# An AdaLN-FFN kernel: byte-packed transposes, weights transposed into SBUF, and new orders on every engine

## What is computed

```python
def fake_quant(x):                      # per row
    s = max(max(|x|) / 127, 1e-8)
    return clip(round(x / s), -127, 127) * s

y = einsum('bij,bkj->bik', x, weight[itok])        # f32 accuracy
h = layernorm(y) * gamma + beta
h = fake_quant(h) @ fake_quant(w1).T + b1
g = gelu(h)
out = x + fake_quant(g) @ fake_quant(w3).T + b3
```

## Time and profile before

| | us |
|---|---|
| median of 3 runs (lowest, highest) | 359.89 (357.31, 361.01) |
| the profiled execution, its own time | 362.2 |
| its span in the trace | 360.4 |
| TensorE busy | 338.1 |
| VectorE, GpSimd, ScalarE busy | 282.6, 264.3, 226.4 |
| mean granted TensorE clock | 0.99 |

### The profile page before, as it was taken

One profiled execution on the slowest core, in us unless ns is written; L12 is line 12 of the kernel. 1 busy time (PEld: TensorE's weight loads), 2 busy tenths in 40 slices (PEclk: granted clock), 3 DMA queues, 4 the chain that ended last, 5 costly groups with the idle time before them and its releaser, 6 DMA issues. The chain is left out here.

```text
span 360.4 us, 5778 instructions
## 1 busy us (share of the span) xinstructions
PE 338.1 (94%) x1854; PEld 234.1 (65%) x1880; DVE 282.6 (78%) x344; ACT 226.4 (63%) x232; POOL 264.3 (73%) x164
## 2 busy tenths in 40 slices
PE   5899999998887999999899999999999999999885
PEld 5788888865753666676665666566666666665442
DVE  0669888879676589798779878788879877979866
ACT  2443668856976567874596468756777478525640
POOL 1503279545997799976999689978997899956840
PEclk9999999999998999999999999999999999999989
DMA  7999986791995399479962999099946990150014
GB/s 240 362 391 411 400 241 122 182 222 56 241 220 128 103 240 215 86 197 260 221 137 87 301 223 202 3 259 260 217 79 166 295 239 0 59 176 1 0 57 177
DMA packets 46203, 67.35 MB, mean 187 GB/s; under 512 B 2918, under 2 KB 37734, under 8 KB 46186
## 3 DMA queue, kind: packets, MB, share of 16 engines
q1 hardware_dynamic: 46186, 67.14, 70.2%
HBM read 58.74 MB, written 8.39 MB: 186 GB/s over the span
## 5 line engine op out<-in xcount | busy, mean ns | idle before, releaser
L1114 PE MATMUL a_ps<-w_hi,x_hi 128*128 128x512 f32 x256 | 106.6, 416 | 1.8 <-ACT y L608 1.7
L1116 PE MATMUL a_ps<-w_hi,x_lo 128*128 128x512 f32 x256 | 100.1, 391 | 0.0
L1115 PE MATMUL a_ps<-w_lo,x_hi 128*128 128x512 f32 x256 | 99.8, 390 | 0.0
L1168 PE MATMUL f_ps<-w_q,q_t 128*128 128x512 bf16 x377 | 89.8, 385 | 3.7 <-ACT q_t L646 2.5
L593 ACT ACTIVATE w_hi<-t_ps 128x1024 fp32r<-128x1024 f32 x48 | 48.3, 1020 | 39.2 <-DVE t_ps L828 39.0
L1168 PEld LDWEIGHTS f_ps<-w_q,q_t 128*128 128x128 bf16 x400 | 37.6, 99 | 51.1 <-issue 7.5
L828 DVE STREAM_TRANSPOSE t_ps<-w_nat 128x1024 f32<-128x1024 f32 x48 | 58.0, 1240 | 14.5 <-DMA w_nat<-in_L_cond_weight 14.4
L834 DVE TENSOR_TENSOR w_lo<-t_ps,w_hi 128x1024 fp32r<-128x1024 f32 x48 | 57.2, 1215 | 4.5 <-ACT w_hi L593 4.3
L1114 PEld LDWEIGHTS a_ps<-w_hi,x_hi 128*128 128x128 f32 x256 | 48.2, 188 | 14.0 <-ACT y L608 3.1
L1116 PEld LDWEIGHTS a_ps<-w_hi,x_lo 128*128 128x128 f32 x256 | 48.0, 188 | 10.6
L1115 PEld LDWEIGHTS a_ps<-w_lo,x_hi 128*128 128x128 f32 x256 | 48.3, 189 | 9.0
(11 more groups left out here) (151 smaller groups left out, 492.1 us busy)
## 6 DMA issues: line engine op xcount, KB each, us to landing
w_nat<-in_L_cond_weight SPq DMA_DIRECT2D x96, 256.0 KB, 6.7
x_res<-in_x SPq DMA_DIRECT2D x7, 1024.0 KB, 7.0
out<-o SPq DMA_DIRECT2D x14, 512.0 KB, 3.0
x_nat<-in_x SPq DMA_DIRECT2D x24, 256.0 KB, 9.6
w_nat<-in_L_cond_weight SPq DMA_DIRECT2D x10, 512.0 KB, 7.2
w_q<-in_L_ffn_w SPq DMA_DIRECT2D x4, 512.0 KB, 10.2
h_r<-in_L_cond_weight SPq DMA_DIRECT2D x4, 512.0 KB, 8.1
w_scale_row<-in_L_ffn_w SPq DMA_DIRECT2D x3, 512.0 KB, 13.3
```

The costliest lines, as they stand in the source:

```text
L1114: pe.matmul(ps, hi, w_hi[:, u, c], start=begin, stop=False)
L1115: pe.matmul(ps, hi, w_lo[:, u, c], start=False, stop=False)
L1116: last = pe.matmul(ps, lo, w_hi[:, u, c], start=False, stop=end)
L1168: last = pe.matmul(ps[:, half, :], q[:, c, :], w[:, c, half_of(half)], start=c == 0, stop=c == CB - 1)
```

## The change

What it does, part by part:

1. **h and g as bytes.** `round_h` and `round_g` write int8 directly (no added constant), into `h_r` viewed as bytes. Two neighbouring bytes are taken as one 16-bit word, so `transpose_tile` needs four blocks in place of eight, and half a bank. `take_h` and `take_g` read the bytes with a stride. Weights keep the old form.
2. **Transposed adapter weights in SBUF.** In the loop `transpose_w` writes `y_first` (SBUF, two buffers) instead of `t_ps`. Both inputs of `low_w` then lie in SBUF, and it is a `scalar_tensor_tensor` with a factor 1.0 in place of a `tensor_tensor`. The same form replaces VectorE's other large sums of two SBUF tensors in the last period.
3. **`t_ps` for the FFN.** Tile 1 of ffn1 and ffn2 uses `t_ps[:, 0]`, h and g transposes use `t_ps[:, 1]`, so tiles 0 and 1 no longer share banks.
4. **Scale rows through DRAM.** `store_scales` writes `wq_scale` to a scratch tensor, `load_scale_row` reads it back broadcast; `scale_row` and `take_scale_row` are gone.
5. **Start.** The first unit's hi·hi matmuls wait only for `w_hi`. DMA issues, TensorE, ScalarE, VectorE and GpSimd are in a new order.
6. **Last period.** New order; its normalisers skip two small instructions; the last half of the last tile is computed, finished and stored in two quarters of 256 columns.

```diff
+            if isinstance(b, int) and b == 2:
+                return t_ps[:, k].rearrange("p b k -> p (b k)").rearrange("p (c n) -> p c n", n=LOADED)
+            return y_first[:, k].rearrange("p (c n) -> p c n", n=LOADED)
...
+            return t_ps[:, 0] if t == 1 and not (isinstance(f, int) and f == 0) else f_ps[:]
...
-                dve.tensor_tensor(part_of_unit(w_lo, u, k), piece_bank(k), part_of_unit(w_hi, u, k).bitcast(F32),
-                                  ALU.subtract).then_inc(w_lo_ready, 1)
+                dve.scalar_tensor_tensor(part_of_unit(w_lo, u, k), piece_buffer(b, k), 1.0,
+                                         part_of_unit(w_hi, u, k).bitcast(F32), ALU.mult, ALU.subtract
+                                         ).then_inc(w_lo_ready, 1)
...
-                act.activation(a[:, t, :], a[:, t, :], ACT.Identity, scale=g_inv[:, t:t + 1], bias=magic[:]
-                               ).then_inc(g_rounded, 1)
+                act.activation(g_8[t], a[:, t, :], ACT.Identity, scale=g_inv[:, t:t + 1]).then_inc(g_rounded, 1)
...
-                for c in range(CB):
-                    last = pe.transpose(blocks[:, c, :], halves[:, c * P:(c + 1) * P], ident_16[:])
+                words = src.bitcast(BF16)
+                for c in range(CB // PACK):
+                    last = pe.transpose(blocks[:, c, :], words[:, c * P:(c + 1) * P], ident_16[:])
...
+                sp.dma_start(scale_scratch[n].rearrange("(i p) -> p i", p=P), wq_scale[:, RT * n:RT * (n + 1)],
+                             allow_slow_non_contiguous=True
+                             ).then_inc(scales_stored[n], 16)
...
+                sp.dma_start(w_scale_row[:, n, :], scale_scratch[n:n + 1, :].broadcast_to([P, D])
+                             ).then_inc(scale_row_loaded[n], 16)
...
             def period(p):
-                piece(p, 2, 0)
                 transpose_h(p - 1, 0)
                 transpose_h(p - 1, 1)
+                piece(p, 2, 0)
                 piece(p, 2, 1)
-                ffn1(p - 1, 0)
                 piece(p, 3, 0)
                 piece(p, 3, 1)
+                ffn1(p - 1, 0)
                 ffn1(p - 1, 1)
                 piece(p + 1, 0, 0)
+                piece(p + 1, 0, 1)
+                piece(p + 1, 1, 0)
                 transpose_g(p - 1, 0)
-                piece(p + 1, 0, 1)
+                piece(p + 1, 1, 1)
+                transpose_g(p - 1, 1)
                 ffn2(p - 1, 0)
-                piece(p + 1, 1, 0)
-                transpose_g(p - 1, 1)
-                piece(p + 1, 1, 1)
                 ffn2(p - 1, 1)
```

More of the change, by code:

```diff
@@ L8 @@
 BF16 = mybir.dt.bfloat16
+I8 = mybir.dt.int8
 I16 = mybir.dt.int16
@@ L130, in adaln_ffn_kernel @@
         x_rows = {0: o, 13: x_last}
+        bytes_of = [h_r[:, t, :].bitcast(I8) for t in range(TT)]
+        h_8 = [row[:, 0:D] for row in bytes_of]
+        g_8 = [row[:, D:2 * D] for row in bytes_of]
+        g_8_last = [row[:, 2 * D:3 * D] for row in bytes_of]
+        scale_scratch = nc.dram_tensor("scale_scratch", (2, D), F32, kind="Internal").ap()
         a_ps = psum("a_ps", [P, TT, BANK])
@@ L982, in rescale_and_bias_half @@
                     dve.wait_ge(last_half_scaled, half + 1)
-                    dve.tensor_tensor(part, part, b1_row[:, half_of(half)], ALU.add).then_inc(last_half_biased, 1)
+                    dve.scalar_tensor_tensor(part, part, 1.0, b1_row[:, half_of(half)], ALU.mult, ALU.add
+                                             ).then_inc(last_half_biased, 1)
                 def max_half(half):
@@ L1117, in products, with first_unit_piece @@
                 return last
+            def first_unit_piece(k):
+                pe.wait_ge(first_hi_ready, first_piece(1, k) + 1)
+                for t in range(TT):
+                    tokens = slice(t * P, (t + 1) * P)
+                    for c in range(CP * k, CP * (k + 1)):
+                        pe.matmul(a_ps[:, t, :], x_hi[:, c, tokens], w_hi[:, 0, c], start=c == 0, stop=False)
+                pe.wait_ge(first_lo_ready, first_piece(1, k) + 1)
+                for t in range(TT):
+                    tokens = slice(t * P, (t + 1) * P)
+                    for c in range(CP * k, CP * (k + 1)):
+                        pe.matmul(a_ps[:, t, :], x_hi[:, c, tokens], w_lo[:, 0, c], start=False, stop=False)
+                        last = pe.matmul(a_ps[:, t, :], x_lo[:, c, tokens], w_hi[:, 0, c], start=False, stop=False)
+                if k == 1:
+                    last.then_inc(w_used, 1)
             def piece(b, u, k):
                 kh, ch = divmod(u, CH)
+                if isinstance(b, int) and b == 0 and u == 0:
+                    first_unit_piece(k)
+                    return
                 if isinstance(b, int) and b == 0:
@@ new lines, in ffn2_last, with ffn2_last_quarter @@
+                def ffn2_last(t, half):
+                    pe.wait_ge(g_t_ready, TT * LAST + t + 1)
+                    if t == 0:
+                        pe.wait_ge(ffn1_scaled, KH * TT * LAST + half + 1)
+                    else:
+                        pe.wait_ge(last_half_scaled, half + 1)
+                    product_half(q_last[:, 1, t], w_q[1], (t_ps[:, 1], f_ps)[t], half, ffn2_done)
+                def ffn2_last_quarter(n):
+                    pe.wait_ge(last_half_scaled, KH)
+                    if n == 1:
+                        pe.wait_ge(last_o_scaled, 1)
+                    for c in range(CB):
+                        last = pe.matmul(last_quarter(n), q_last[:, 1, 1, c, :],
+                                         w_q[1][:, c, D - BANK // 2 * (2 - n):D - BANK // 2 * (1 - n)],
+                                         start=c == 0, stop=c == CB - 1)
+                    last.then_inc(ffn2_done, 1)
@@ L1376, in _ @@
             prepare((13,))
-            piece(2, 0, 1)
+            piece(2, 0, 0)
             prepare((14,))
             prepare((15,))
+            piece(2, 0, 1)
+            transpose_g(0, 0)
             piece(2, 1, 0)
-            scale_row(1)
+            ffn2(0, 0)
             piece(2, 1, 1)
-            transpose_g(0, 0)
-            ffn2(0, 0)
             transpose_g(0, 1)
```

614 lines of the change are left out of this document (344 added, 270 removed).

## The result

The changed kernel takes 390.07 us (median of 4 runs, 389.55 to 392.99), the kernel before 358.6 on the same chip: ratio 1.085 [1.080, 1.090]. I had said 343, faster. It is slower by 31 us, and outside my range, which went up to 368.

The account below looks back on a forecast made before the run. A loop period was taken as TensorE's own work plus about 1.1 us of waiting. 362.2 - 5.2 (start) - 6.5 (five periods) - 5.1 (last period) - 0.7 (last store) = 344.7, less 2.3, 342.4; said 343, range 336 to 368.

Parts of the forecast that it names:

- the middle kind: Loop, `low_w`: only GpSimd instructions beginning inside one wait; 1.6 us a period for GpSimd, 0.4 us charged to the period.
- My own bounds: Loop, eight `low_w` a period: cost between nothing and 7.0 us of GpSimd plus 16.8 us of VectorE.
- the other pair: Last period of the old trace: two VectorE `tensor_tensor`, 4.53 us against 2 x 1.2, waited about 2.1 us for GpSimd.
- The second rival: Loop: shared reads of `low_w` slow GpSimd, period 42 us, median 365; with VectorE waiting too 43.5 and 373; chance 0.20.
- The list of TensorE: Loop: TensorE's own work in a period, 37.6 us before, falls by 0.9 to 36.7 us.
- Bytes at 0.9 us a period: Loop: four transposed blocks instead of eight for each of four tiles take 0.9 us a period off TensorE.
- The 0.3 and 0.4 us: Loop: waits added per period, 0.3 us for ScalarE's late chain, 0.4 for GpSimd slowed by `low_w`; period 37.4 us.
- The start: Before the loop: -1.9 scale rows, -0.9 bytes, -2.6 waits, -1.7 slow stretch, +1.9 `prepare` steps and conversions; sum -5.2 us.
- the lower bound: Start, scale rows through DRAM: the scatter's price lies between nothing and the start's whole gain; nothing was taken.
- The last period: From 309.34: -1.8 transposes, -2.7 wait for `take_g`, -1.6 slow clock, 1.0 given back for the new order; -5.1 us.
- The last store: End: it waits for a quarter of the columns instead of half, saving about half of VectorE's 0.75 and 0.69: -0.7 us.
- The transpose into SBUF: Loop, VectorE: 1.14 us per 1024 elements against 1.24 into PSUM, 0.8 us less in a period.

Follow-up runs that it names:

- experiment 2: Changed kernel with `low_w` in the loop as `tensor_tensor` instead of `scalar_tensor_tensor`, both operands in SBUF: 392.79 us (one run).
- experiment 1: Changed kernel with the second operand of `low_w` in the loop read from a stale PSUM quarter instead of `w_hi` (`w_lo` wrong): 356.29 us, ratio 0.987.
- experiment 4: Changed kernel with GpSimd's elementwise operations in the loop cut to 8 columns, `low_w` still on two SBUF operands: 349.19 us (one run).
- experiment 6: Kernel before with h and g as bytes alone: 358.98 us, ratio 0.991; with the weights' columns permuted to match, 360.01 us, ratio 0.999.
- experiment 7: Kernel before with h and g as bytes and the scale rows through DRAM, orders as before: 366.65 us, ratio 1.017.
- experiment 8: Kernel before with bytes and scale rows through DRAM, the scale stores moved so that no load waits behind the scales on SP: 367.6 us, ratio 1.018.
- experiment 9: Changed kernel with the second `low_w` operand from PSUM in the loop and `residual_last` behind the last tile's first `rescale1_half`: 354.15 us, ratio 0.985.

## Why the prediction was wrong

**The step that failed** is the one I called disputed, `low_w`: "I take the middle kind: a GpSimd instruction that begins inside a `low_w` waits for its end, one that is running is not disturbed", 1.6 us a period, hidden. In its place: both directions hold (timelines above), `low_w` takes 2.28 us and not 1.2, and the two engines' times add up. The period is 43.75 instead of 37.4, and 5 x 6.35 = 32 us of the miss of 47 are this one step, the slow clock behind the waits included. My own bounds had it: "nothing, or 0.87 us of GpSimd and 2.1 us of VectorE for each of eight, 7.0 and 16.8 us a period". Measured are some 5 us of GpSimd (39.00 against 34.05) and 8.6 of VectorE (8 x 1.07), and I booked 1.6 and nothing.

The rows I had said enough. I read the 1.31 us of the `scalar_tensor_tensor` as proof that it is not held. But no GpSimd instruction was running at 317.79, so there was nothing to be held by; timeline of GpSimd there:

```profile
314.26 3.27 POOL L478 TENSOR_TENSOR o<-o,x_res 128x1024 f32<-128x1024 f32 x1
317.83 0.19 POOL L450 TENSOR_TENSOR var_eps<-mean_var,eps 128x1 f32<-128x1 f32 x1 [0.30 <-DVE mean_var L944]
```

One row is not explained: `var_eps` begins 0.04 us inside the `scalar_tensor_tensor` and still takes its usual 0.19 us, so the sentence that the trace agrees "in every meeting that it has" goes a little too far; at such a distance the records may not tell who came first. The 2.1 us that the other pair had lost I did not carry over, because its form was another, and experiment 2 shows that both forms are held. And I priced collisions by chance (3.6 of 14, half of 0.87 each) where the right question was whether two engines' work fits one after the other: 34.1 us of GpSimd and 9.7 of `low_w` are 43.8, more than any list in the kernel. The second rival had the place and, "with VectorE waiting too, 43.5 us", the size of the period; it gave 373 in all because it kept my gains elsewhere. Its first figure, 42 us, counts only GpSimd's loss and is too low. The rule of the Trainium skill ("SBUF — State Buffer", section "Who interferes with whom") that I quoted agrees with these runs (2.28 us shared, 1.21 alone), and I gave the rival that follows it 0.20.

**The list of TensorE**, 36.7 us: right, 36.79 in experiments 1 and 4. Bytes at 0.9 us a period: right as work (it is in the 36.79), but in the old orders little or nothing of it is left (experiment 6). That the new orders turn it into time is only seen together with them; no run has the orders without the bytes. The 0.3 and 0.4 us that I added for ScalarE and GpSimd did not show.

**The start**, -5.2, came out at +0.5. I counted what TensorE loses and nothing that its loads lose: the swap of the first loads, not in my list at all, up to 2.0 us; the scale rows, where I took the lower bound, "nothing", 3.5 us of VectorE's wait and 2.5 of TensorE's, more behind the second store. Experiments 7 and 8 put their price at 6 to 7 us in the old orders, against the -1.9 that I booked; both ends of my bound were too kind. Which part of the 5.7 us belongs to which is open: the same start ends up to 4 us apart from run to run, and in experiment 1 the two waits are 1.19 and 0.24 us.

**The last period**, -5.1, came out at +0.6: the long wait for `take_g` did go, but `residual_last`, held for 6.8 us, and the sums behind it made TensorE wait 3.9 us for `round_h`; experiment 9 gets about 2 us back. **The last store**, -0.7, came out at +1.7: by the timeline a final sum took 1.99 us in place of 0.69 because GpSimd was adding `x_res`, and VectorE then stood 2 us behind TensorE, with two short instructions for each quarter; this part is read from the trace, no run tests it. **The transpose into SBUF**, "1.14 us", takes 1.23: no gain over PSUM's 1.24.

## What to carry to other kernels

When a change moves an operand from PSUM to SBUF, add up the times of VectorE's instructions with two SBUF inputs and of GpSimd's work, and compare the sum with the period; a price per meeting misleads. Add what TensorE loses to a lower clock behind the waits that come of it. An undisturbed duration in a trace is evidence only if the other engine was running then: look up what it did in the same microseconds. A small transfer that replaces work on the bottleneck is to be priced by what stands behind it in its queue and by the loads that move at the same time, not by its bytes.

## What the runs showed of the hardware

A VectorE instruction with both inputs in SBUF and a GpSimd elementwise instruction did not run at the same time in the meetings looked at: 2.28 us instead of 1.21 and up to 3.3 for GpSimd instead of 2.39, in `tensor_tensor` and `scalar_tensor_tensor` alike; with one input from PSUM they take 1.21 and 2.39. Behind waits of 3.5 us TensorE's granted clock was 0.50 for up to 5.2 us, and its matmuls started 0.43 us apart instead of 0.23. A DMA that scatters 1024 single words (4 KB) from SBUF to DRAM took 12.1 to 14.0 us from issue to landing, about twice as long as a 256 KB load of adapter weights (5.5 to 7.1 us in the same runs; 256 KB loads of x take about 10). A 32 x 32 block transpose of 1024 elements per partition takes 1.23 us into SBUF and 1.24 into PSUM.
